# Rotated keys summed on TensorE: cosine and sine part multiplied by the identity into one PSUM bank

## The chip, the cores and the metric

The kernel runs on one core of one Trainium2 chip. The metric is the device time of one execution in microseconds. Three executions of the kernel before took 4159.46 us in the median, 4158.87 us at the least and 4160.84 us at the most.

## What is computed

The input is `x` of shape (8, 512, 128), float32. A modulation vector made from `c` gives shifts, scales and gates. First comes a full attention block with dense 512 x 512 scores for each of the 8 batches. Then comes a stack of six layers, each a windowed attention with rotary positions and a feed-forward part; this stack takes nearly all of the time. Cut to what the change touches:

```python
def attn_layer(x, Wqkv, qs, ksc, Wo):          # x is (8, 512, 128); 16 heads of 64
    q, k, v = split(x @ Wqkv)                  # three times 1024 columns
    q = l2norm(q) * qs
    k = l2norm(k) * ksc
    q = q * cos * scale + rotate_half(q) * sin * scale
    k = k * cos / scale + rotate_half(k) * sin / scale
    out = local_attention(q, k, v)             # windows of 32, each also sees the one before
    return out @ Wo

for i in range(6):
    x = attn_layer(shift_tokens(x), ...) + x
    x = ffn_layer(shift_tokens(x), ...) + x
```

The rotated keys are the sum of a cosine part and a sine part. Tokens lie on partitions when that sum is made, and the scores need the head dimension on partitions, so queries and keys are both turned by TensorE afterwards.

## The kernel before

The stack works on tiles of 128 tokens: 4 tiles in a batch, 32 in a layer, 192 in all. Five engine programs (SyncE, TensorE, ScalarE, GpSimd, VectorE) run side by side and meet only at semaphores. Each is a list of steps per slot, written out by hand for four kinds of slot (`c % 4`). The first slots and the last are unrolled, and the rest is a hardware loop over groups of four slots (`slots`, L276), which goes round 45 times and branches back once for four tiles. A step with lag 2 in slot c works on tile c - 2, so a tile passes through several slots, and each engine's own order decides what can be late.

Per tile, TensorE does six projections (`proj`, L533: chunks 0 and 1 are the queries, 2 and 3 the keys, 4 and 5 the values; each is one float32 matmul of 512 columns into bank 0 or 1). It then does 16 transposes of the rotated queries and keys (`qk_back`, L541: parts 0 and 1 are queries, 2 and 3 keys, four 128 x 128 blocks each, into bank 2 or 5), the mask and 128 small score matmuls (`scores`, L550 and L557), the weighted values (`pv`, L571 and L578, into banks 2 and 5 too) and the output projection (`out_proj`, L589). Once per batch come the centring matmul (L597), transposes of the normalised rows (`norm_back_ffn`, L605), six feed-forward matmuls (`ffn_in`, L613) and three that close it (`ffn_out`, L621).

ScalarE copies the banks out (`to_raw` L1128, `to_v` L1142, `qk_to_sbuf` L1153, `o_to_sbuf` L1164), squares (L1136) and takes the exponentials (L1158) and the gelu (L1187), between which its table is loaded anew. VectorE sums the squares (L1585), scales by the norm (`normed`, L1592), makes the cosine part into `rot` (`cos_part`, L1602) and adds the sine part (`rotated`, L1609), each on 128 x 1024 elements, once for queries and once for keys. It also does the softmax (L1546 to L1571) and the 32 x 32 transpose of the probabilities (`probs_back`, L1578). GpSimd makes the norm's inverse root (L1325, L1327) and the sine part into `swp` (`sin_part`, L1337). SyncE moves the transposed probabilities to a block-diagonal tile `PT` with eight DMAs a tile (`bands`, L356 to L361), for which `pv` waits; `PT` has one buffer, so `bands` also waits for the `pv` of the tile before.

In every slot of the kernel before TensorE runs its steps in nearly this order: `proj` 1 and 3, `qk_back` 1, `out_proj` (lag 4), `qk_back` 0, `proj` 0, `qk_back` 3 and 2, `proj` 4 and 5 (lag 3), `scores` (lag 2), `proj` 2, `pv` (lag 3). In the last kind of slot (`c % 4 == 3`) `norm_back_ffn` follows `pv`, and then the loop turns.

Of the kernel before, what the change touches and what calls it, by code (L numbers as in the profile page):

```python
# [7 lines left out]
ALU = mybir.AluOpType  # L8
# [9 lines left out]
P = 128  # L18
# [49 lines left out]
def adaln_block(nc, x_d, wq_d, wk_d, wv_d, wo_d, bq_d, bk_d, bv_d, bo_d, cT_d, wmod_d,  # L68
# [3 lines left out]
    with ctx:  # L72
# [99 lines left out]
        RAW_BANK = (0, 0, 1, 1, 1, 0)  # L172
# [65 lines left out]
        rot_ready = [sem(f"rot_ready{i}") for i in range(2)]  # L238
# [85 lines left out]
        def _(sp):  # L324
# [68 lines left out]
            def loads_and_moves(l):  # L393
                load_wqkv(l, 1)
                load_wqkv(l, 3)
                load_wqkv(l, 0)
# [3 lines left out]
                move(l, -2)  # L400
                move(l, -1)
                load_wqkv(l, 4)
                load_wqkv(l, 5)
# [22 lines left out]
        def _(pe):  # L426
# [86 lines left out]
            def after(k, c, lag, out):  # L513

                if type(k) is int:
                    wait(pe, out, min(c - lag + 1, NI))
                else:
                    pe.wait_ge(out, k * TPB + (c - lag + 1))

            def after_batch(k, c, lag, out, base=0):  # L520

                b = k + (c // TPB - lag)
                if type(k) is int:
                    if b >= 0:
                        pe.wait_ge(out, min(b, NB - 1) + 1 + base)
                else:
                    pe.wait_ge(out, b + (1 + base))
# [8 lines left out]
            def qk_back(n, b, j, i):  # L536

                pe.wait_ge(rot_ready[i // 2], n + 1)
                for u in range(4):
                    col = (4 * i + u) * P  # L540
                    mm = nc.tensor.transpose(bank[QK_BANK[i]][:, u * P:(u + 1) * P], rot[:, col:col + P], ident[:, :])  # L541
# [82 lines left out]
            def slot(k, c):  # L624
                if c % TPB == 0:
                    if type(k) is int:
                        after(k, c, 1, raw_out[0])
                    if type(k) is int:
                        after(k, c, 1, raw_out[1])
                    after(k, c, 4, v_out[1])  # L630
                    step(k, c, 0, proj, 1, 0)
                    if type(k) is int:
                        after(k, c, 4, v_out[0])
                    if type(k) is int:
                        after(k, c, 1, raw_out[3])
                    after(k, c, 1, raw_out[2])
                    step(k, c, 0, proj, 3, 1)
                    if type(k) is int:
                        after(k, c, 3, qkT_out[3])
                    if type(k) is int:  # L640
                        after(k, c, 3, qkT_out[1])
                    after(k, c, 4, oT_out)
                    step(k, c, 2, qk_back, 1)
                    step(k, c, 4, out_proj)
# [6 lines left out]
                    if type(k) is int:  # L651
                        after(k, c, 4, v_out[1])
                    if type(k) is int:
                        after(k, c, 1, raw_out[0])
                    after(k, c, 0, raw_out[1])
                    step(k, c, 0, proj, 0, 0)
                    if type(k) is int:
                        after(k, c, 4, oT_out)
                    if type(k) is int:
                        after(k, c, 3, qkT_out[3])  # L660
                    after(k, c, 2, qkT_out[1])
                    step(k, c, 2, qk_back, 3)
# [6 lines left out]
                    if type(k) is int:  # L669
                        after(k, c, 1, raw_out[2])  # L670
                    if type(k) is int:
                        after(k, c, 4, v_out[0])
                    after(k, c, 0, raw_out[3])
                    step(k, c, 3, proj, 4, 1)
                    if type(k) is int:
                        after(k, c, 0, raw_out[1])
                    if type(k) is int:
                        after(k, c, 4, v_out[1])
                    after(k, c, 0, raw_out[0])
                    step(k, c, 3, proj, 5, 0)  # L680
# [17 lines left out]
                    step(k, c, 2, scores)  # L698
                    if type(k) is int:
# [15 lines left out]
                    if type(k) is int:  # L715
                        after(k, c, 0, raw_out[3])
                    if type(k) is int:
                        after(k, c, 1, raw_out[2])
                    after(k, c, 3, v_out[0])
                    step(k, c, 0, proj, 2, 1)  # L720
# [16 lines left out]
                    if type(k) is int:  # L737
                        after(k, c, 2, qkT_out[0])
                    if type(k) is int:
                        after(k, c, 4, oT_out)  # L740
                    if type(k) is int:
                        after(k, c, 2, qkT_out[1])
                    after(k, c, 2, qkT_out[2])
                    after(k, c, 2, qkT_out[3])
                    step(k, c, 3, pv)
# [16 lines left out]
                elif c % TPB == 1:  # L762
                    if type(k) is int:
                        after(k, c, 1, raw_out[0])
                    if type(k) is int:
                        after(k, c, 1, raw_out[1])
                    after(k, c, 4, v_out[1])
                    step(k, c, 0, proj, 1, 0)
                    if type(k) is int:
                        after(k, c, 4, v_out[0])  # L770
                    if type(k) is int:
                        after(k, c, 1, raw_out[3])
                    after(k, c, 1, raw_out[2])
                    step(k, c, 0, proj, 3, 1)
                    if type(k) is int:
                        after(k, c, 3, qkT_out[3])
                    if type(k) is int:
                        after(k, c, 3, qkT_out[1])
                    after(k, c, 4, oT_out)
                    step(k, c, 2, qk_back, 1)  # L780
                    step(k, c, 4, out_proj)
                    if type(k) is int:
                        after(k, c, 3, qkT_out[2])
                    if type(k) is int:
                        after(k, c, 3, qkT_out[0])
# [971 lines left out]
```

## Time and profile before

| what | value |
|---|---|
| median of 3 executions | 4159.46 us |
| profiled execution, its own time | 4191.03 us |
| its span, first to last instruction | 4189.0 us |
| mean granted TensorE clock | 0.921 of 2.4 GHz |
| busy share: TensorE, VectorE, GpSimd, ScalarE | 83%, 82%, 66%, 54% |
| first maximum of the softmax (first tile of the stack) | 329.7 us |
| last maximum of the softmax (tile 192) | 4064.3 us |

The profiled execution is 31.6 us (0.8%) longer than the median; shares and durations are read from it, and a change is carried over to the median in proportion. The busy time of TensorE counts modelled ends of matmuls, so what one step costs it is read from the start of one group of matmuls to the start of the next. Idle time of an engine matters only where the end waits for that engine.

### The profile page before, as it was taken

The numbers are of one execution on the slowest core, as the hardware profiler recorded it, in microseconds if no ns is written. First come the engines' busy times: TensorE is split into PE (matmuls) and PEld (weight loads), VectorE is DVE, ScalarE is ACT, GpSimd is POOL, SyncE is SP. The second block draws the span as 40 slices with busy tenths as digits, with TensorE's granted clock in tenths as the row PEclk, the third lists the DMA queues.
The fourth block names the chain that finished last, engine by engine and source line by source line (L and its number), as shares of the span: only waits on it lengthen the run. The fifth ranks groups of instructions, "written<-read, shape, count | busy, mean of one in ns | idle before, by whom it ended". The sixth has DMA issues, their size and how long they took to land. (4 is left out here: it accounts for less than half of the span.)

```text
span 4189.0 us, 120019 instructions
## 1 busy us (share of the span) xinstructions
PE 3460.1 (83%) x45916; PEld 2280.4 (54%) x46108; DVE 3441.1 (82%) x3850; ACT 2249.0 (54%) x3593; POOL 2757.9 (66%) x2144
## 2 busy tenths in 40 slices
PE   4667888888888888888888888888888888888873
PEld 2334555555555555555555555555555555555551
DVE  4658888888888888888888888898898888888871
ACT  2434555555555555555555555555655555655541
POOL 3027767777766776777766767777777767767740
PEclk8779999999999999999999999999999999999985
DMA  1001111111111111111111111111111111111110
GB/s 57 0 0 32 27 27 31 28 37 46 28 27 28 31 37 43 31 27 32 27 37 43 31 27 29 30 37 47 27 31 27 27 39 45 27 31 28 27 32 20
DMA packets 104466, 129.72 MB, mean 31 GB/s; under 512 B 34508, under 2 KB 48208, under 8 KB 104016
## 3 DMA queue, kind: packets, MB, share of 16 engines
q1 hardware_dynamic: 104016, 122.49, 12.0%
q8 instruction: 432, 7.08, 0.7%
q14 instruction: 18, 0.15, 0.0%
HBM read 19.62 MB, written 2.10 MB: 5 GB/s over the span
## 5 line engine op out<-in xcount | busy, mean ns | idle before, releaser
L533 PE MATMUL bank<-wqkv,xs 128*128 128x512 f32 x2304 | 1209.0, 632 | 81.8 <-issue 71.9
L1337 POOL TENSOR_TENSOR swp<-raw,TS 128x512 f32<-128x512 f32 x768 | 960.8, 1272 | 392.4 <-DVE raw L1592 392.1
L1327 POOL TENSOR_TENSOR rr<-ssm,nhalf 128x16 f32<-128x16 f32 x384 | 1176.2, 3063 | 32.0
L1128 ACT ACTIVATE raw<-bank 128x512 f32<-128x512 f32 x768 | 436.9, 597 | 641.2 <-PE bank L533 641.1
L571 PE MATMUL mid<-PT,V 128*64 128x128 f32 x6144 | 462.6, 314 | 298.1 <-DMA PT<-PTd 298.0
L571 PEld LDWEIGHTS mid<-PT,V 128*64 128x64 f32 x6144 | 409.9, 160 | 453.8 <-DMA PT<-PTd 358.9
L533 PEld LDWEIGHTS bank<-wqkv,xs 128*128 128x128 f32 x2304 | 400.1, 197 | 362.6 <-issue 347.7
L1592 DVE TENSOR_TENSOR raw<-raw,rr 128x1024 f32<-128x1024 f32 x384 | 472.0, 1229 | 144.6 <-POOL rr L1327 144.6
L1347 POOL COPY kT<-kT 128x256 f32<-128x256 f32 x192 | 194.7, 1014 | 545.9 <-ACT kT L1153 545.8
L541 PEld LDWEIGHTS mid<-ident,rot 128*128 128x128 f32 x3072 | 379.3, 144 | 248.8 <-issue 228.4
L1609 DVE TENSOR_TENSOR rot<-rot,swp 128x1024 f32<-128x1024 f32 x384 | 468.5, 1220 | 30.1 <-POOL swp L1337 3.5
L1602 DVE TENSOR_TENSOR rot<-raw,TC 128x1024 f32<-128x1024 f32 x384 | 462.0, 1203 | 11.4 <-PE mid L541 10.8
L1585 DVE TENSOR_REDUCE ss<-sq 128x16 f32<-128x1024 f32 x384 | 464.9, 1211 | 5.1 <-ACT sq L1136 5.1
L541 PE MATMUL mid<-ident,rot 128*128 128x128 f32 x3072 | 446.2, 277 | 0.8 <-ACT qT L1153 0.4
L1164 ACT ACTIVATE OT<-mid 128x512 f32<-128x512 f32 x384 | 208.4, 595 | 428.6 <-PE mid L578 296.9
L1136 ACT ACTIVATE sq<-raw 128x1024 f32<-128x1024 f32 x384 | 406.0, 1057 | 29.9 <-DVE ss L1585 14.4
L589 PE MATMUL bank<-OT,fwo 128*128 128x128 f32 x3072 | 381.8, 278 | 3.0 <-ACT OT L1164 3.0
L589 PEld LDWEIGHTS bank<-OT,fwo 128*128 128x128 f32 x3072 | 366.8, 196 | 3.1 <-issue 3.1
L1153 ACT ACTIVATE qT<-mid 128x512 f32<-128x512 f32 x384 | 231.4, 603 | 182.0 <-PE mid L541 182.0
L557 PEld LDWEIGHTS mid<-kT,qT 64*32 64x32 f32 x24576 | 277.5, 105 | 90.1 <-issue 83.6
L613 PE MATMUL bank<-xnT,w 128*128 128x512 f32 (+1 forms) x576 | 315.0, 629 | 8.3 <-ACT ge L1187 4.3
L557 PE MATMUL mid<-kT,qT 64*32 64x64 f32 x24576 | 315.4, 226 | 1.8 <-issue 1.8
(128 smaller groups left out, 4393.1 us busy)
## 6 DMA issues: line engine op xcount, KB each, us to landing
PT<-PTd SPq DMA_DIRECT2D x1344, 64.0 KB
BT<-PTd SPq DMA_DIRECT2D x192, 64.0 KB
wqkv<-d_wqkv SPq DMA_DIRECT2D x36, 256.0 KB, 2.7
fwo<-d_fwo SPq DMA_DIRECT2D x6, 512.0 KB, 4.0
d_out<-X SPq DMA_DIRECT2D x8, 256.0 KB, 2.3
w<-d_w SPq DMA_DIRECT2D x6, 341.0 KB
w<-d_w SPq DMA_DIRECT2D x6, 128.0 KB
wmod<-d_wmod SPq DMA_DIRECT2D x1, 384.0 KB, 3.3
```

Of the source, the lines that this page charges most:

```text
L533: nc.tensor.matmul(bank[bk][:, :], xs[:, j, :], wqkv[:, c, :], start=True, stop=True)\
L541: mm = nc.tensor.transpose(bank[QK_BANK[i]][:, u * P:(u + 1) * P], rot[:, col:col + P], ident[:, :])
L557: mm = nc.tensor.matmul(bank[3 + h][w * W:(w + 1) * W, u * DH:(u + 1) * DH], qT[r, j % 2, u, w * W:(w + 1) * W], kT[r, j % 2, u, w * W:w * ...
L571: mm = nc.tensor.matmul(OUT_BANK[u // 4][h * DH:(h + 1) * DH, (u % 4) * P:(u % 4 + 1) * P], V[:, j % 2, hc:hc + DH], PT[:, :, h * HH + u, ...
L589: mm = nc.tensor.matmul(bank[6][:, j * P:(j + 1) * P], fwo[:, c, :], OT[:, c, :], start=(c == 0), stop=(c == HH - 1), skip_group_check=True)
L1128: nc.scalar.activation(raw[:, j % 2, c * 512:(c + 1) * 512], bank[RAW_BANK[c]][:, :], ACT.Copy)\
L1327: pool.tensor_tensor(rr[:, s], ssm[:, s], nhalf[:, s], ALU.pow).then_inc(rr_ready[i], 1)
L1337: last = pool.tensor_tensor(dst[:, :, t, :], src[:, :, 1 - t, :], tab.broadcast_to([P, HEADS, 32]), ALU.mult)
L1585: nc.vector.tensor_reduce(ss[:, s], sq[:, :].rearrange("p (h d) -> p h d", d=DH), AX.X, ALU.add).then_inc(ss_ready[i], 1)
L1592: nc.vector.tensor_tensor(q, q, rr[:, s].unsqueeze(2).broadcast_to([P, HEADS, DH]), ALU.mult)\
L1602: nc.vector.tensor_tensor(rot[:, i * INNER:(i + 1) * INNER].rearrange("p (h d) -> p h d", d=DH), q, tab.broadcast_to([P, HEADS, DH]), ALU. ...
L1609: nc.vector.tensor_tensor(rot[:, r], rot[:, r], swp[:, r], ALU.add).then_inc(rot_ready[i], 1)
```

## The change

The sum of the rotated keys leaves VectorE. `rotated` stays for the queries; for the keys TensorE multiplies each 128 x 128 block of `rot` by the identity, and then the block of `swp` by the identity into the same place of the same bank, which turns and adds at once. The semaphores follow: `rot_ready` is one, `qk_back` 2 and 3 wait for the cosine and the sine part, and GpSimd's `sin_part` for the keys waits until TensorE has read `swp`.

With it the order of the steps is written anew on every engine. `pv` moves from lag 3 at the end of the slot to lag 4 after the first two projections. `scores` is the last step of TensorE's slot in the kinds 0, 2 and 3, and `norm_back_ffn` goes to the first kind of slot, so that the loop turns right behind `scores`. On ScalarE the exponentials move to lag 3 and the output copy to lag 4. On VectorE the cosine part of the queries and the key norm move to the next slot, ahead of the maximum. On GpSimd the sine part of the queries moves to lag 2. SyncE loads the weight chunks in another order.

```diff
-        RAW_BANK = (0, 0, 1, 1, 1, 0)
+        RAW_BANK = (1, 0, 1, 1, 0, 0)
...
-        rot_ready = [sem(f"rot_ready{i}") for i in range(2)]
+        rot_ready = sem("rot_ready")
...
                 load_wqkv(l, 1)
+                load_wqkv(l, 0)
                 load_wqkv(l, 3)
-                load_wqkv(l, 0)
                 move(l, -4)
                 load_wqkv(l, 2)
                 move(l, -3)
                 move(l, -2)
+                load_wqkv(l, 5)
                 move(l, -1)
                 load_wqkv(l, 4)
-                load_wqkv(l, 5)
...
             def qk_back(n, b, j, i):
 
-                pe.wait_ge(rot_ready[i // 2], n + 1)
+                if i < 2:
+                    pe.wait_ge(rot_ready, n + 1)
+                else:
+                    pe.wait_ge(cos_ready[1], n + 1)
+                    pe.wait_ge(sin_ready[1], n + 1)
                 for u in range(4):
                     col = (4 * i + u) * P
-                    mm = nc.tensor.transpose(bank[QK_BANK[i]][:, u * P:(u + 1) * P], rot[:, col:col + P], ident[:, :])
+                    dst = bank[QK_BANK[i]][:, u * P:(u + 1) * P]
+                    if i < 2:
+                        mm = nc.tensor.transpose(dst, rot[:, col:col + P], ident[:, :])
+                    else:
+                        nc.tensor.matmul(dst, rot[:, col:col + P], ident[:, :], start=True, stop=False)
+                        mm = nc.tensor.matmul(dst, swp[:, col:col + P], ident[:, :], start=False, stop=True)
                 mm.then_inc(qkT_done[i], 1)
```

TensorE's slot of the kind `c % 4 == 3` after the change, its steps alone (the waits for free banks between them are left out); the kind 2 is the same without `centred`:

```python
step(k, c, 0, proj, 1, 0)
step(k, c, 0, proj, 0, 1)
step(k, c, 4, pv)
step(k, c, 3, proj, 5, 0)
step(k, c, 0, proj, 3, 1)
step(k, c, 2, qk_back, 3)
step(k, c, 2, qk_back, 0)
step(k, c, 4, out_proj)
step(k, c, 2, qk_back, 1)
step(k, c, 2, qk_back, 2)
step(k, c, 3, proj, 4, 0)
batch(k, c, 1, centred)
step(k, c, 0, proj, 2, 1)
step(k, c, 2, scores)
```

The kind 0 has `norm_back_ffn` (lag 2) after `pv`, and `ffn_in` 0 of the gate between `proj` 2 and `scores`. The kind 1 has the other five `ffn_in` after `proj` 1, `proj` 0, `pv`, `proj` 3 and `qk_back` 2, and `ffn_out` after `scores`.

```diff
             def sin_part(n, b, j, i):
 
                 pool.wait_ge(qn_ready[i], n + 1)
-                wait(pool, rot_ready[i], n)
+                if i == 0:
+                    wait(pool, rot_ready, n)
+                else:
+                    for c in (2, 3):
+                        wait(pool, qkT_done[c], n)
...
             def rotated(n, b, j, i):
                 dve.wait_ge(sin_ready[i], n + 1)
                 dve.wait_ge(cos_ready[i], n + 1)
-                r = slice(i * INNER, (i + 1) * INNER)
-                nc.vector.tensor_tensor(rot[:, r], rot[:, r], swp[:, r], ALU.add).then_inc(rot_ready[i], 1)
+                r = slice(0, INNER)
+                nc.vector.tensor_tensor(rot[:, r], rot[:, r], swp[:, r], ALU.add).then_inc(rot_ready, 1)
```

The other engines' slots after the change, kind 2, steps alone (ScalarE, GpSimd, VectorE):

```python
to_raw 1, to_raw 0, exps (lag 3), o_to_sbuf (lag 4), squares 0, qk_to_sbuf 3, qk_to_sbuf 0 (lag 2),
to_raw 3, to_v 5 (lag 3), qk_to_sbuf 1, qk_to_sbuf 2 (lag 2), to_raw 2, to_v 4 (lag 3), squares 1
take_x, sin_part 0, sin_part 1 (lag 2), norms 0 (lag 1), keys_before (lag 2), norms 1 (lag 1)
sumsq 0, cos_part 0, normed 1, rotated 0 (lag 1), maxes, less_max (lag 2), cos_part 1 (lag 1),
sumsq 1, sums, sums_inverse, probs (lag 2), normed 0, probs_back (lag 2), x_between
```

In the kind 0 ScalarE's three gelus stand at the end of its slot, behind `squares` 1.

## Rows read from the trace of the kernel before

**Rows 1.** The page, busy time: us, share of span, instructions, of TensorE.

```profile
PE 3460.1 (83%) x45916; PEld 2280.4 (54%) x46108; DVE 3441.1 (82%) x3850; ACT 2249.0 (54%) x3593; POOL 2757.9 (66%) x2144
```

**Rows 2.** Windows, the stack: length, busy of PE, PEld, DVE, ACT, POOL, clock, DMA.

```profile
330.00:4064.00 3734.00, 3227.49 (x45037) 2153.89 (x45227) 3241.18 (x3370) 2105.14 (x3322) 2673.10 (x1994) 0.95 0.14 32
```

**Rows 3.** Waits of TensorE: who waited for whom, us in total, times, longest.

```profile
PE mid L571 <- DMA PT<-PTd: 298.0, 114, 6.3
PE bank L533 <- issue: 71.9, 49, 2.7
PE mid L550 <- ACT kT L1153: 66.5, 51, 5.5
...
PE bank L621 <- DVE ge L1640: 35.1, 47, 1.3
```

**Rows 4.** Groups by line: shapes, count, busy us and mean ns, idle before.

```profile
L1609 DVE TENSOR_TENSOR rot<-rot,swp 128x1024 f32<-128x1024 f32 x384 | 468.5, 1220 | 30.1 <-POOL swp L1337 3.5
...
L1128 ACT ACTIVATE raw<-bank 128x512 f32<-128x512 f32 x768 | 436.9, 597 | 641.2 <-PE bank L533 641.1 <-DVE rot L1602 0.2
...
L1136 ACT ACTIVATE sq<-raw 128x1024 f32<-128x1024 f32 x384 | 406.0, 1057 | 29.9 <-DVE ss L1585 14.4
...
L589 PE MATMUL bank<-OT,fwo 128*128 128x128 f32 x3072 | 381.8, 278 | 3.0 <-ACT OT L1164 3.0
...
L1187 ACT ACTIVATE ge<-bank,b 128x512 f32<-128x512 f32 x144 | 98.8, 686 | 108.6 <-PE bank L613 108.0
...
L1187 ACT ACT_TABLE_LOAD x48 | 61.6, 1283 | 0.8
```

**Rows 5.** Timeline of TensorE's matmuls, 2054 to 2058 us: start, length, line, count.

```profile
2054.20 1.95 PE L589 MATMUL bank<-OT,fwo 128*128 128x128 f32 x16
2055.98 0.60 PE L541 MATMUL mid<-ident,rot 128*128 128x128 f32 x4
2056.42 1.02 PE L533 MATMUL bank<-wqkv,xs 128*128 128x512 f32 x2
2057.28 1.04 PE L541 MATMUL mid<-ident,rot 128*128 128x128 f32 x8
```

**Rows 6.** Line 276, the loop: ns min/median/max, first and last start; PEldq, ACTq sequencers.

```profile
L276 PEldq COMPARE_BRANCH  x45: 76/3557/3887, 580.1 to 4027.7; - x45
...
L276 ACTq COMPARE_BRANCH  x45: 40/45/45, 582.2 to 4030.7; - x45
```

**Rows 7.** Timeline of TensorE around the loop's first turn.

```profile
578.66 2.84 PE L571 MATMUL mid<-PT,V 128*64 128x128 f32 x28
581.43 0.66 PE L605 MATMUL bank<-ident,xn 128*128 128x128 f32 x4
583.89 1.59 PE L533 MATMUL bank<-wqkv,xs 128*128 128x512 f32 x2 [1.81 <-issue]
```

**Rows 8.** Timeline of TensorE, end of a slot of kind 3 and the next.

```profile
2536.84 0.38 PE L550 MATMUL mid<-maskb,identb 128*128 128x512 bf16 x1 [0.33 <-issue]
2537.15 1.58 PE L557 MATMUL mid<-kT,qT 64*32 64x64 f32 x128
2538.66 1.13 PE L533 MATMUL bank<-wqkv,xs 128*128 128x512 f32 x2
2543.59 3.63 PE L571 MATMUL mid<-PT,V 128*64 128x128 f32 x32 [3.81 <-DMA PT<-PTd]
...
2549.64 2.98 PE L533 MATMUL bank<-wqkv,xs 128*128 128x512 f32 x4 [1.83 <-issue]
```

**Rows 9.** Windows: `pv` after that wait; columns as in Rows 2.

```profile
2543.60:2546.90 3.30, 3.30 (x32) 3.25 (x32) 3.20 (x3) 1.06 (x1) 3.13 (x3) 0.51 0.03 5
```

**Rows 10.** Timeline of VectorE: the probabilities' transpose, and two steps in a row.

```profile
2534.94 1.25 DVE L1578 STREAM_TRANSPOSE PTd<-Pr 128x1024 f32<-128x1024 f32 x1
...
2597.39 1.22 DVE L1592 TENSOR_TENSOR raw<-raw,rr 128x1024 f32<-128x1024 f32 x1
2598.53 1.21 DVE L1585 TENSOR_REDUCE ss<-sq 128x16 f32<-128x1024 f32 x1
```

## What I predicted, and how it was worked out

> **What bounds the kernel now.** I first read the page's busy shares: TensorE and VectorE are both at 82% to 83%, GpSimd at 66%, so neither of the first two can be taken for the bound by its share [rows 1]. Over the stack alone, 3734 us, TensorE is busy 3227 us and VectorE 3241 us, 86% and 87% [rows 2]. TensorE therefore has 507 us in which its array does nothing, and that is the number against which this change must be held, since the change gives TensorE work and takes it from VectorE.
>
> The waits say where these 507 us lie [rows 3]. `pv` waits 298 us for the DMAs that fill `PT`, the loop's first projection 72 us for "issue", the mask matmul before `scores` 67 us for the key copy, and the last feed-forward matmul 35 us for VectorE. The timeline shows one such end of slot: `scores`, a projection, then 3.81 us of nothing until `pv`, and 1.83 us more before the next slot's projection [rows 8]. Between these stalls TensorE is gapless. So it is a chain through TensorE (scores, softmax on VectorE, eight DMAs, `pv`, then TensorE's next slot) that sets the period, with TensorE 86% full.
>
> The granted clock is 0.95 over the stack [rows 2]. The levels are 2.4 and 1.2 GHz, so 3734 x 0.05 x 2 = 373 us ran at the lower one. It falls behind the long wait: after the 3.81 us gap the `pv` ran at 0.51 for 3.3 us [rows 8, 9].
>
> **The keys' work on TensorE.** Eight key blocks a tile were one transpose each; now each is two float32 matmuls. What a transpose costs is read between starts: four from 2055.98 to 2056.42, 0.110 us each [rows 5]. For the new matmul the nearest row is `out_proj`, with the same shape: 128x128 stationary, 128 columns moving, float32. It has 3072 instructions for 192 x 8 matmuls, so two per matmul, and 16 of them took 2054.20 to 2055.98, 0.111 us each [rows 4, 5]. A block now costs 4 x 0.111 = 0.445 us in place of 0.110. That is 0.335 us more, and with 192 x 8 = 1536 blocks **+515 us**. From the other side, if float32 times the identity went through in one instruction as a transpose does, a block would cost 0.222 us and the term would be +172 us. I take +515, by the row of equal kind.
>
> **The addition taken from VectorE.** 192 of the 384 executions of line 1609 go, at 1.14 us from start to start (1.22 us long, overlapping) [rows 4, 10]: 219 us of VectorE. I cost them at nothing. VectorE would have 3241 - 219 = 3022 us of work in a stack that TensorE alone fills for longer; this takes more idle from VectorE than there was, but no wait of TensorE that the new order would not also take.
>
> **The new order.** `pv` of a tile ran one slot after its scores; now it runs early in the second. After `scores` come on VectorE nine steps and a reciprocal until `probs_back` ends, about 10.2 us by 1.14 to 1.25 us each [rows 4, 10]. From the end of `probs_back` (2536.19) to the waiting `pv` it took 7.4 us, DMA issue and landing together [rows 8, 10]. So `pv` could start 17.6 us after `scores` ends. TensorE reaches it after one whole slot and two projections of 0.86 us [rows 5]. A plain slot now sums to 16.7 us: six projections (5.2), `pv` (3.0: its first 32 matmuls half of the 3.63 us at the lower clock, and an estimated 1.1 for the 32 small ones, whose price lies between the 0.012 us of a score matmul and the 0.057 us of a wide one), two key parts (3.56), two query parts (0.88), `out_proj` (1.78), `scores` with the mask (2.3) [rows 5, 8]. That makes 18.4 us, later than 17.6, and the slots with feed-forward work are longer. So **-298 us**, with a cover of only 0.8 to 2 us in plain slots; if VectorE comes late, part returns. The mask's wait for the key copy goes too, since two projections now stand between the last key part and `scores`. Of its 66.5 us, 51 x 0.33 us stay, a gap that the row shows without any wait [rows 3, 8]: **-50 us**. The last feed-forward matmul now stands behind `scores`, with its input ready: **-35 us** [rows 3]. The other waits in the new slot I covered one by one. The bank copies of 0.60 us lie behind `pv`, `out_proj` or two projections. `qk_back` 3 needs the cosine part made four steps after the previous `scores` ended, before the slot's first five steps (6.5 us) are over. `sin_part` and `keys_before` have GpSimd's spare third.
>
> The gelus lose cover. The first follows `proj` 2 on ScalarE by a copy, another copy, squares, a table load and itself: 0.60 + 0.60 + 1.06 + 1.28 + 0.69 us [rows 4], with 0.4 us of hand-over 4.6 us. TensorE has 0.9 (`ffn_in`) + 2.3 + 0.9 us = 4.1 us to fill, and waits 0.5 us. The second gelu has one projection, 0.86 us, against 0.69 + 0.4 us, and costs 0.25 us. With 48 batches this makes **+36 us**, between 0 and +60. The weight loads in another order cost nothing: each has most of a slot before its chunk is used, as before. Pipeline fill and drain have the same 8 slots; I leave 10 us either way for them.
>
> **The turn of the loop.** TensorE's sequencer takes 3.56 us (median of 45) for the loop's branch, ScalarE's 0.045 us [rows 6]. In the first turn the branch started at 580.1 and the next projection at 583.89, 3.8 us later. Work already queued covered part: the rest of `pv` and the four transposes, up to 582.1, so 1.81 us stood open [rows 6, 7]; the mean is 71.9 / 45 = 1.6 us. Wide work hid the rest. In the new order the branch follows `scores`, 128 matmuls in 1.5 us, 0.012 us each [rows 8]. A queue holding the same 18 matmuls or so that still ran during the old turn (four transposes and 14 of `pv`) now hides 0.2 us. So 3.6 us stand open, 2.0 us more, 45 times: **+90 us**. The bounds are 0, if the branch is reached as early in time as now, and +100.
>
> The Trainium skill (Runtime: NRT & Kernel Launch, Instruction fetch mechanics) says that a taken branch whose target lies outside the two pages of instructions at hand waits for a DMA fetch; the 3.56 us on TensorE against 0.045 us on ScalarE agree. Another page of the Trainium skill (Advanced Engine Details and Errata, Control Flow Timing) gives a compare-and-branch 108 ns; here TensorE's trace contradicts it.
>
> **The clock.** Today the low stretches cost about half of 373 us where TensorE works, 86% of it: 160 us. They follow the `pv` gaps, which go: **-160 us**. But the new gap of 3.6 us at the turn is nearly the 3.81 us behind which the clock fell. I take it that it falls for 3.4 us once in a turn, as in rows 9, and half of that is lost: 45 x 1.7 = **+76 us**, between 0 and +150.
>
> The Trainium skill (TensorE: Matmul & The Clock Gate, Part 4) holds that transposes do not count as activity for the clock as matmuls do. By it the change feeds the clock, and the +76 us would be 0; no row here parts the two.
>
> **The sum:** 515 - 298 - 50 - 35 + 36 + 90 - 160 + 76 = +174 us. On 4191.03 us of the profiled execution this gives 4365 us, and on the median 4159.46 x 4365 / 4191.03 = **4332 us**, 4.1% slower. The change fills TensorE's idle time and then some.
>
> **Rivals.** *The turn costs TensorE nothing* (the other side). If the branch took no array time, its +90 and +76 and today's 72 us would go: 174 - 90 - 76 - 72 = -64 us, 4096 us. It decides from the point where less than about 1.4 us of a turn stands open. Control Flow Timing, named above, would give this. Against it stand 45 turns of the same length. With one instruction a matmul (+172 in place of +515) the sum is -169 us, 3992 us, but two rows of instructions per matmul speak against it. Together 0.08.
>
> *The turn stays as now and the clock holds:* 174 - 90 - 76 = +8 us, 4167 us, no change. Chance 0.05. *Only one of the two holds:* +84 to +98 us, 4243 to 4257 us. Chance 0.17.
>
> *`PT` comes late again.* The cover is 0.8 to 2 us in plain slots, and VectorE's own order has waits for TensorE in it (the gated products in the kind 0 slot wait for `ffn_in` while the softmax stands behind them). With 2 us lost in two slots of each batch, +190 us: 174 + 190 = +364 us, 4521 us; with a half of it 4426 us. Chance 0.20.
>
> *The change doesn't do what it says:* if VectorE kept 384 additions, nothing of the sum would change but VectorE's load; the diff leaves no room for it.
>
> **How the numbers follow.** Forecast, 4332 us, with its own range 4290 to 4385: 0.50. No more than 2 in 10 may be left out: I go from 4190, above the cases of no change and of the other side (0.13), to 4470, which takes most of the late-`PT` case. About 0.2% is what a measurement of this kernel can tell from no change. Faster: 0.08. Same: 0.05. Slower: 0.50 + 0.17 + 0.20 = 0.87.
>
> **What would show it.** In the changed kernel's groups by line, line 1609 has 192 executions, and the key matmuls have 6144 instructions, near 0.111 us from start to start. TensorE's busy share over the stack rises to nine tenths. Its waits hold little on `PT`, and "issue" before the first projection is near 45 x 3.6 = 160 us. The granted clock is below 1 once in four tiles, behind the turn. I am wrong if `PT` waits stay above 100 us, if the turn is as open as before, or if the key matmuls go at half the price.

## The result

| kernel | median | against the kernel before, same chip |
|---|---|---|
| before | 4160.15 us (4 runs, that chip) | |
| changed | 4359.5 us (4357.85 to 4362.37) | 1.0474 [1.0455, 1.0493] |

The change makes the kernel 4.7% slower. The profiled execution of the changed kernel took 4359.32 us, with a span of 4357.3 us against 4189.0 us: 168 us more. Between the medians it is 199 us, since the profiled execution of the kernel before was 31.6 us above its median and that of the changed kernel was at its own.

From its page, the busy times, and from the windows one window of the stack (length, busy PE, PEld, DVE, ACT, POOL, clock, DMA share, GB/s). These answer rows 1 and 2:

```profile
PE 3910.7 (90%) x50716; PEld 2736.4 (63%) x50716; DVE 3412.3 (78%) x3658; ACT 2249.5 (52%) x3593; POOL 2848.1 (65%) x2144
...
330.00:4064.00 3734.00, 3472.57 (x47033) 2461.74 (x47033) 3033.89 (x3002) 1990.75 (x3141) 2616.97 (x1890) 0.97 0.13 31
```

TensorE went from 86% to 93% of the stack and VectorE from 87% to 81%. TensorE's waits in the changed kernel, answering rows 3 (us in total, times, longest):

```profile
PE bank L534 <- issue: 175.9, 48, 5.4
PE mid L581 <- DMA PT<-PTd: 59.0, 53, 5.2
...
PE bank L623 <- ACT ge L1197: 20.1, 48, 1.1
PE mid L550 <- ACT OT L1174: 20.0, 36, 0.9
...
PE mid L567 <- issue: 8.5, 21, 0.9
...
PE bank L631 <- DVE ge L1654: 1.3, 1, 1.3
```

The wait for `PT` fell from 298 to 59 us, those before the mask and the last feed-forward matmul are gone, and the turn of the loop rose from 72 to 176 us. Its place in TensorE's timeline (start, length, line, count), the branch's own line (ns min, median, max; first and last start), and two windows, the empty array and the projection after the turn, answering rows 6 to 9:

```profile
2565.99 1.93 PE L567 MATMUL mid<-kT,qT 64*32 64x64 f32 x128
2571.82 3.58 PE L534 MATMUL bank<-wqkv,xs 128*128 128x512 f32 x4 [3.90 <-issue]
...
L276 PEldq COMPARE_BRANCH  x45: 76/3602/5071, 570.3 to 4240.7; - x45
...
570.80:574.00 3.20, 0.00 (x0) 0.00 (x0) 3.20 (x3) 0.06 (x1) 3.04 (x3) 1.00 0.10 26
574.50:578.00 3.50, 3.50 (x10) 1.24 (x11) 3.50 (x3) 1.61 (x5) 3.33 (x4) 0.55 0.02 5
```

The branch lasts as long as before, 3.60 us, and nothing stands over it. After it the clock is at its lower level, 1.2 GHz, for a stretch.

The matmuls that were added, from the timeline of one key part, which answers rows 5:

```profile
2561.07 0.39 PE L550 MATMUL mid<-ident,rot 128*128 128x128 f32 x2
2561.29 0.39 PE L551 MATMUL mid<-ident,swp 128*128 128x128 f32 x2
...
2562.63 0.39 PE L551 MATMUL mid<-ident,swp 128*128 128x128 f32 x2
2562.85 1.02 PE L534 MATMUL bank<-wqkv,xs 128*128 128x512 f32 x2
```

Sixteen instructions from 2561.07 to 2562.85, 0.111 us each.

One difference lies outside the stack. At the end, the chain that ended last (start, us, what) shows this in the kernel before and then in the changed one:

```profile
4130.23 44.07 issue
4174.30 1.10 PE bank L1056 x4
```

```profile
4342.28 0.30 issue
4342.59 1.10 PE bank L1066 x4
```

In those 44 us the trace of the kernel before holds 404 semaphore instructions on TensorE's queue and no matmul. All but one are waits that `after` and `after_batch` emit in unrolled slots whose steps have run out, each long satisfied, one every 0.109 us. In the diff of the change these two helpers have new conditions, `if c - lag < NI` and `if 0 <= b < NB`, which no longer emit them. So the stack itself became 168 + 44 = 212 us longer, not 168. From the first to the last maximum of the softmax it is 3735 us before and 3953 us (325.1 to 4277.9) after.

### The profile page after: what moved, and what is told of

Its sections match the earlier page's. It is cut to its first block and busy times, and to the rows that moved or that the text cites. A ratio compares the mean times of both kernels' runs of the same rounds, so it can differ in the third digit from the quotient of the medians.

```text
span 4357.3 us, 128635 instructions
## 1 busy us (share of the span) xinstructions
PE 3910.7 (90%) x50716; PEld 2736.4 (63%) x50716; DVE 3412.3 (78%) x3658; ACT 2249.5 (52%) x3593; POOL 2848.1 (65%) x2144
## 5 line engine op out<-in xcount | busy, mean ns | idle before, releaser
L534 PE MATMUL bank<-wqkv,xs 128*128 128x512 f32 x2304 | 1200.8, 639 | 179.8 <-issue 175.9
L1351 POOL TENSOR_TENSOR swp<-raw,TS 128x512 f32<-128x512 f32 x768 | 1119.4, 1487 | 0.4 <-DVE raw L1606 0.4
L1327 POOL COPY xs<-F 128x128 f32 (+1 forms) x192 | 178.1, 928 | 1051.2 <-issue 856.7
L1623 DVE TENSOR_TENSOR rot<-rot,swp 128x1024 f32<-128x1024 f32 x192 | 386.3, 2012 | 410.2 <-POOL swp L1351 410.2
L550 PE MATMUL mid<-ident,rot 128*128 128x128 f32 x3072 | 600.4, 277 | 26.2 <-ACT OT L1174 20.0
L551 PE MATMUL mid<-ident,swp 128*128 128x128 f32 x3072 | 595.9, 276 | 0.0
L550 PEld LDWEIGHTS mid<-ident,rot 128*128 128x128 f32 x3072 | 479.1, 192 | 135.6 <-issue 70.0
L581 PEld LDWEIGHTS mid<-PT,V 128*64 128x64 f32 x6144 | 355.7, 144 | 238.8 <-issue 152.8
L1163 ACT ACTIVATE kT<-mid 128x512 f32<-128x512 f32 x384 | 229.3, 597 | 481.0 <-PE mid L551 481.0
L551 PEld LDWEIGHTS mid<-ident,swp 128*128 128x128 f32 x3072 | 468.4, 193 | 0.0
L581 PE MATMUL mid<-PT,V 128*64 128x128 f32 x6144 | 402.3, 287 | 59.0 <-DMA PT<-PTd 59.0
L623 PE MATMUL bank<-xnT,w 128*128 128x512 f32 (+1 forms) x576 | 311.5, 623 | 25.0 <-ACT ge L1197 20.1
```

The lines of the kernel that those rows point to most:

```text
L534: nc.tensor.matmul(bank[bk][:, :], xs[:, j, :], wqkv[:, c, :], start=True, stop=True)\
L550: nc.tensor.matmul(dst, rot[:, col:col + P], ident[:, :], start=True, stop=False)
L551: mm = nc.tensor.matmul(dst, swp[:, col:col + P], ident[:, :], start=False, stop=True)
L581: mm = nc.tensor.matmul(OUT_BANK[u // 4][h * DH:(h + 1) * DH, (u % 4) * P:(u % 4 + 1) * P], V[:, j % 2, hc:hc + DH], PT[:, :, h * HH + u, ...
L1351: last = pool.tensor_tensor(dst[:, :, t, :], src[:, :, 1 - t, :], tab.broadcast_to([P, HEADS, 32]), ALU.mult)
```

## The experiments

The theory on record: TensorE binds the changed kernel; its work, the open turn and the clock behind the turn cost time one to one. The general rival: the new order of steps, or another engine, sets the time. The order of the sections is that in which the runs were made; each group of sections that names one comparison ran against its own runs of the kernel before, so ratios are compared, and a difference of ratios is given in us of 4160.

The 44 us at the end must be kept apart. The kernels made from the kernel before (it and the experiments 4, 8 and 11) have them, all the others don't. Where the two sorts are compared, 44 us (0.011) of the difference of the ratios is not the sum of the keys and not the order of the stack. The profiles give the stack alone, from the first to the last maximum:

| kernel | stack, us |
|---|---|
| before | 3735 |
| changed | 3953 |
| addition back, new order | 3831 |
| matmuls, old order | 3907 |
| before, loop written out | 3729 |
| changed, loop written out | 3742 |
| addition back, new order, loop written out | 3747 |
| matmuls, old order, loop written out | 3812 |
| all three together | 3558 |

### The turn moved behind wide work

```diff
-            slots(pe, 8, slot)
+            slots(pe, 10, slot)
```

> The changed kernel with TensorE's loop shifted by two slots, so that it turns behind ffn_out (six wide matmul instructions, 2.65 us) and no longer behind scores. No work is added or left out. My theory: the turn stands open on TensorE's path. In the changed kernel 45 turns wait 175.9 us in all, 3.9 us each; behind ffn_out about 2.5 us of each should be hidden (-112 us), and with an opening of about 1.4 us the clock should mostly not fall behind it (about -60 us): near 4190 us, between 4170 and 4260. Rival, the turn lies beside other waits (the order of the other engines sets the period): no change, 4340 to 4370 us.

Measured: 4293.68 us, 1.0286 [1.0265, 1.0307]. That is 0.0188 less than the changed kernel, 78 us. Half of what I expected.

```profile
PE bank L534 <- issue: 122.4, 78, 2.5
...
PE mid L550 <- ACT OT L1174: 33.7, 88, 1.0
PE bank L615 <- ACT xn L1183: 32.9, 41, 4.4
...
L276 PEldq COMPARE_BRANCH  x44: 83/4384/4748, 611.7 to 4137.4; - x44
```

The first three rows are TensorE's waits, the last the branch. The turn does lie on the path, so the rival falls. But the branch itself now lasts 4.38 us instead of 3.60, and two ScalarE waits that the long stall had covered came out.

### The keys' cosine part alone

```diff
-                        nc.tensor.matmul(dst, rot[:, col:col + P], ident[:, :], start=True, stop=False)
-                        mm = nc.tensor.matmul(dst, swp[:, col:col + P], ident[:, :], start=False, stop=True)
+                        mm = nc.tensor.transpose(dst, rot[:, col:col + P], ident[:, :])
```

> The changed kernel, but TensorE makes four transposes of rot a key part as the kernel before did and leaves the keys' sine part out of the result; all waits stay. It takes away the added TensorE work alone (0.335 us a block, 515 us in all) and adds nothing elsewhere. My theory, TensorE's work is the bound: the time falls by 515 us until something else binds. A plain slot would be 14.0 us, and pv can start only 17.6 us after scores; one slot and two projections are then 15.7 us, so some 1.9 us of waiting for PT come back in most slots, about +240 us: near 4085 us, between 3900 and 4130. Rival, the order of the steps on VectorE and GpSimd made the changed kernel slow and the matmuls are hidden: above 4300 us.

Measured: 4123.45 us, 0.9879 [0.9858, 0.9899]; 248 us less than the changed kernel for 515 us less TensorE work. Its waits and its branch:

```profile
PE bank L534 <- issue: 214.3, 49, 5.4
PE mid L580 <- DMA PT<-PTd: 175.5, 52, 5.0
...
L276 PEldq COMPARE_BRANCH  x45: 76/4590/5130, 558.5 to 4006.6; - x45
```

The time is inside my range. The added work is on the path, and the cover of `PT` that I had put at 0.8 us in plain slots is thin: with 2.7 us less work a tile, 116 us of waiting for `PT` return. Another 38 us went into a longer branch. The granted clock of the stack was 0.94 (330 to 4050 us) in place of 0.97, which is 0.03 x 2 x 3720 = 223 us more at the lower level, half of it lost: some 110 us. With these three, what is left of the 515 us is the 248 us measured.

### The addition back on VectorE, in the new order

```diff
+                pe.wait_ge(rot_ready[i // 2], n + 1)
...
+                        mm = nc.tensor.transpose(dst, rot[:, col:col + P], ident[:, :])
...
                     step(k, c, 1, cos_part, 1)
+                    step(k, c, 1, rotated, 1)
```

> The changed kernel's order of steps, but the keys' sum is made as in the kernel before: an addition on VectorE right behind the keys' cosine part, then transposes. My theory: as with the cosine part alone, but the addition (1.15 us) stands between the maximum and the probabilities of the same slot and lengthens the way from scores to pv: near 4200 us, between 4080 and 4280, so faster than the changed kernel by TensorE's 515 us less what comes back as waiting. Rival, the new order itself is what costs: 4360 us or more, since VectorE has more to do.

Measured: 4237.62 us, 1.0160 [1.0132, 1.0188].

```profile
PE bank L534 <- issue: 217.6, 52, 5.1
PE mid L576 <- DMA PT<-PTd: 187.3, 55, 4.8
PE mid L546 <- DVE rot L1614: 59.3, 52, 3.3
```

As expected: in the new order the matmuls cost 131 us more than the addition that they replace. Even so this kernel stays slower than the kernel before, so the new order alone, with the same arithmetic, costs 1.6%. In the stack it costs more, 97 us (3831 against 3735), since only the kernel before has the 44 us at the end. The waits show where: 218 us before the loop's first projection, in place of 72. A part of that is a longer branch, 4.67 us in the median.

### The matmuls in the old order

```diff
-                pe.wait_ge(rot_ready[i // 2], n + 1)
+                if i < 2:
+                    pe.wait_ge(rot_ready[0], n + 1)
+                else:
+                    pe.wait_ge(cos_ready[1], n + 1)
+                    pe.wait_ge(sin_ready[1], n + 1)
...
-                    step(k, c, 1, rotated, 1)
```

> The kernel before with its own order of steps and its own place of the loop's turn, but with the keys' sum made by the matmuls and VectorE's addition for the keys gone. My theory: TensorE's added 515 us first fill its waits for PT (298 us) and keep the clock up (up to 160 us): near 4220 us, between 4180 and 4350, so faster than the changed kernel by about what the open turn and the clock behind it cost. Rival, only the new order makes room for the matmuls: 4360 us or more.

Measured: 4371.03 us, 1.0475 [1.0447, 1.0504]. My expectation failed: the whole time is the changed kernel's, not 140 us less. But this kernel has the 44 us at the end, and its stack is 46 us shorter than the changed kernel's (3907 against 3953), a third of what I expected.

```profile
PE bank L533 <- issue: 115.6, 49, 3.0
PE mid L559 <- ACT kT L1162: 62.8, 51, 1.8
PE mid L566 <- issue: 50.7, 43, 2.0
...
PE mid L580 <- DMA PT<-PTd: 25.5, 24, 6.3
```

The first half of the thought was right: the wait for `PT` fell from 298 to 26 us. But the waits before `scores` stay, 63 us for the key copy. There are 51 us of new idle time within the score matmuls, 43 times, at places where the program has no wait (why was not tried). And the turn opens wider, 116 us in place of 72. The new order removes those waits and pays for it with a turn of 176 us and the clock behind it; with the loop it loses 46 us by this in the stack, and only the shorter end of the program makes the two times equal.

### TensorE's loop written out

```diff
+        class K(int):
+            pass
...
+            for k in range(1, groups):
+                for i in range(TPB):
+                    body(K(k), lag + i)
...
-            slots(pe, 8, slot)
+            unrolled(8, slot)
```

> The changed kernel with TensorE's loop written out: the same steps and waits in the same order with constants in place of the register, and no turn at all; the other engines keep their loops. My theory: the 176 us of open turns and the some 70 us of lower clock behind them are on the path. With the turn only moved, about 50 us came back as waits for ScalarE (the output copy and the normalised rows), so I expect near 4165 us, between 4100 and 4210. Rival, the sequencer must fetch the same instructions anyway and the stall moves into the straight code: above 4290 us.

Measured: 4143.51 us, 0.9912 [0.9895, 0.9928]. TensorE's waits in the stack and the window of it:

```profile
PE mid L594 <- issue: 56.2, 57, 1.7
...
PE mid L594 <- DMA PT<-PTd: 14.5, 9, 5.9
...
330.00:4000.00 3670.00, 3539.82 (x48868) 2529.20 (x48868) 3156.17 (x3124) 2059.53 (x3266) 2797.38 (x1966) 1.00 0.13 32
```

234 us less than the changed kernel, and inside my range. The projections wait 2.0 us in all for issue in place of 176, the clock is 1.00 over the stack, and TensorE is busy 96%. The turns with the clock behind them are the whole of the slowdown. (The edit also takes the register arithmetic off TensorE's queue. It was not tried alone, but outside the turns the changed kernel's TensorE waited only some 10 us for issue.) But without them the change doesn't make the stack faster either: it takes 3742 us against 3735. The 0.9% (37 us) by which the whole kernel is faster than the kernel before is no more than the 44 us at the end.

### Half the price for a key block

```diff
-                        nc.tensor.matmul(dst, rot[:, col:col + P], ident[:, :], start=True, stop=False)
-                        mm = nc.tensor.matmul(dst, swp[:, col:col + P], ident[:, :], start=False, stop=True)
+                        nc.tensor.transpose(dst, rot[:, col:col + P], ident[:, :])
+                        mm = nc.tensor.matmul(dst, swp[:, col:col + P], ident[:, :], start=False, stop=True,
+                                              skip_group_check=True)
```

> The changed kernel, but the cosine part of a key block is transposed (one instruction) and only the sine part is multiplied by the identity onto it (two). The whole result is computed. A block costs 0.109 + 0.223 = 0.332 us in place of 0.446, 175 us less in all. My theory, the time follows TensorE's work one to one: near 4190 us, between 4160 and 4260. Rival, at this load waits between the engines take over: above 4290 us.

Measured: 4292.97 us, 1.0270 [1.0253, 1.0287]; 85 us less than the changed kernel, not 175.

```profile
PE bank L534 <- issue: 231.6, 48, 5.7
PE mid L582 <- DMA PT<-PTd: 80.5, 52, 5.2
...
L276 PEldq COMPARE_BRANCH  x45: 76/5020/5475, 562.6 to 4174.8; - x45
```

This is outside my range of 4160 to 4260 and just inside the rival's, but it was not mainly waits between the engines that took over. The branch grew to 5.02 us, and that ate 56 us; 22 us went into waiting for `PT`, and the granted clock of the stack was 0.96 in place of 0.97. By the two waits alone 97 us of the 175 us are left, 12 more than measured.

### The addition back, loop written out

The third experiment and the fifth together; no further edit.

> The changed kernel's order with VectorE's addition and the transposes, and TensorE's loop written out. With the loop it took 4238 us, 218 us of it open turns and some 60 us of clock behind them, 187 us waits for PT. My theory: the turns' time goes, and a third of it comes back as waiting for PT: near 4050 us, between 3950 and 4130, faster than the kernel before. Rival, VectorE's chain from scores to pv sets the period and the turn lies inside its shadow: above 4190 us.

Measured: 4158.31 us, 0.9955 [0.9938, 0.9971]: 85 us less than with the loop, well above my 4050 and outside my range, but below the rival's 4190.

```profile
PE mid L589 <- issue: 181.0, 95, 4.1
PE mid L559 <- DVE rot L1627: 136.9, 97, 3.3
PE bank L631 <- DVE ge L1658: 66.6, 49, 1.8
```

Here TensorE waits again: before `pv`, which needs `PT`, and for VectorE before the query parts and the feed-forward matmuls. VectorE is busy 3401 of the 3670 us from 330 to 4000, 93%, and TensorE 87%; VectorE in its turn waits 173 us for GpSimd's sine part, so that VectorE alone binds is likely but not shown. Without turns matmuls (0.9912) and addition (0.9955) are nearly equal in the new order.

### The kernel before, loop written out

The fifth experiment's edit on the kernel before.

> The kernel before with TensorE's loop written out, nothing else changed. Its turns are open 72 us in all and the clock falls again behind a half of them. My theory: the turn stands on the chain through TensorE here too: near 4080 us, between 4040 and 4120. Rival, the wait for PT is the fixed point and takes the gain: within 10 us of the kernel before.

Measured: 4182.33 us, 0.9994 [0.9976, 1.0012]. The rival held.

```profile
PE mid L584 <- issue: 307.8, 123, 4.7
...
PE mid L584 <- DMA PT<-PTd: 36.9, 12, 7.9
```

The waits before `pv` rose from 298 to 345 us. The 72 us of open turns in the kernel before cost nothing: 47 us of them reappear before `pv`, and 37 us of idle time appear within the score matmuls, where there was 2 us.

### Half the price, loop written out

The fifth and the sixth together.

> The changed kernel with TensorE's loop written out, and each key block as one transpose of the cosine part and one matmul of the sine part onto it. The whole result is computed. Without turns the first gain of 175 us can't be eaten by a longer turn. My theory: against the 4144 us of the unrolled kernel, the 175 us go and some 40 us come back as waits for PT and for ScalarE: near 4010 us, between 3960 and 4070, faster than both kernels. Rival, something else already binds the unrolled kernel beside TensorE (VectorE's chain, as in the unrolled kernel with the addition, 4158 us): above 4110 us.

Measured: 4029.89 us, 0.9661 [0.9637, 0.9684], 104 us less than unrolled alone and inside my range.

```profile
PE mid L595 <- issue: 102.9, 86, 2.1
...
PE mid L595 <- DMA PT<-PTd: 17.6, 8, 5.6
```

With no branch to grow, the cheaper block pays, less 50 us that come back before `pv` (121 us against 71).

### The keys' sine part after the queries' addition

VectorE's additions had become longer. The changed kernel's line, what VectorE waited for before it (us, times), and one tile from the timelines of TensorE, VectorE and GpSimd:

```profile
L1623 DVE TENSOR_TENSOR rot<-rot,swp x192: 1209/2268/2285, 307.1 to 4258.2; 128x1024 f32<-128x1024 f32 x192
...
  POOL swp L1351: 410.2, 155
...
2546.86 1.48 PE L567 MATMUL mid<-kT,qT 64*32 64x64 f32 x128
...
2549.61 2.29 DVE L1623 TENSOR_TENSOR rot<-rot,swp 128x1024 f32<-128x1024 f32 x1 [2.64 <-POOL swp L1351]
...
2560.39 1.24 DVE L1592 STREAM_TRANSPOSE PTd<-Pr 128x1024 f32<-128x1024 f32 x1
...
2547.08 5.95 POOL L1351 TENSOR_TENSOR swp<-raw,TS 128x512 f32<-128x512 f32 x4
```

The addition starts when the queries' sine part is done, and at that moment GpSimd starts the keys'. There is a second thing in these lines. In the kernel before the addition waited 3.5 us in all for GpSimd; now, with the queries' sine part moved to lag 2, it waits 410 us. In this tile the scores end at 2548.34, the addition starts 1.3 us later and takes 2.29 us, and `probs_back` ends at 2561.63. That is 13.3 us after the scores, where I had counted 10.2. The experiment parts the addition from the keys' sine part, which starts later by it; the addition's wait for GpSimd stays (407 us).

```diff
                 if i == 0:
                     wait(pool, rot_ready, n)
                 else:
+                    pool.wait_ge(rot_ready, n + 1)
                     for c in (2, 3):
                         wait(pool, qkT_done[c], n)
```

> The changed kernel with TensorE's loop written out, and one wait more on GpSimd: the keys' sine part starts only when the queries' addition on VectorE is done. In the changed kernel the two run side by side in most tiles and take 2.27 us each, against 1.22 and 1.27 us alone. My theory: the addition falls to 1.22 us, and the time stays within 15 us of the unrolled kernel's (4144 us), since TensorE binds. Rival, VectorE's lost microsecond a tile is on the path: 4100 us or less.

Measured: 4083.28 us, 0.9784 [0.9759, 0.9809], 53 us less than unrolled alone. The rival held.

```profile
L1637 DVE TENSOR_TENSOR rot<-rot,swp x192: 1210/1226/1227, 306.9 to 3990.2; 128x1024 f32<-128x1024 f32 x192
...
PE mid L594 <- issue: 17.3, 28, 1.8
...
PE mid L594 <- DMA PT<-PTd: 11.0, 6, 5.4
```

The addition is back at 1.23 us, and the waits before `pv` fell by 42 us (56.2 + 14.5 against 17.3 + 11.0). The additions became 151 us shorter in all (192 of 2.01 us in the mean against 192 of 1.22), and 53 us of that arrived. So VectorE's time between `scores` and `probs_back` reaches TensorE in part, through `PT`, even when TensorE is busy 96% of the time. What the wait for GpSimd costs was not tried.

### The matmuls in the old order, loop written out

The fourth and the fifth together.

> The kernel before in its own order, the keys' sum by matmuls, TensorE's loop written out. With the loop it took 4371 us, 116 us of it before the loop's first projection. My theory after the last runs: with TensorE's added work it is TensorE that binds in this order too, so the turns count here though they did not in the kernel before: near 4250 us, between 4210 and 4290, and thus slower than the new order unrolled (4144 us) by its waits for the key copy. Rival, its own order's waits take the gain as in the kernel before: above 4330 us.

Measured: 4275.64 us, 1.0252 [1.0226, 1.0278], inside my range.

```profile
PE mid L593 <- issue: 101.7, 82, 2.5
PE mid L572 <- ACT kT L1175: 62.9, 51, 1.8
```

93 us less than with the loop, where the kernel before gained nothing from the same edit: with the matmuls TensorE binds in the old order too. Without turns the whole kernel in the new order is 0.034, 141 us, faster. In the stack it is 70 us (3742 against 3812), about the 63 us of waits for the key copy; the 44 us at the end, which this kernel still has, are most of the rest.

### All three together

> The changed kernel with TensorE's loop written out, one transpose and one matmul a key block, and the keys' sine part on GpSimd held until the queries' addition is done. The whole result is computed. Without the last the kernel took 4030 us, with 103 us of issue waits and 18 us of DMA waits before pv. My theory: the collision of VectorE and GpSimd delays the probabilities, and through PT it costs TensorE some 45 to 90 us here, since TensorE has less work to hide it: near 3970 us, between 3940 and 4000. Rival, at this load the later sine part is late for the key blocks and eats the gain: 4020 us or more.

Measured: 3962.66 us (5 runs), 0.9538 [0.9523, 0.9553], 4.6% faster than the kernel before and inside my range. It is 0.0123, 51 us, less than without the held sine part. Of the 190 us, 44 us are again the end of the program; the stack is 177 us shorter (3558 against 3735).

```profile
330.00:3860.00 3530.00, 3395.87 (x47697) 2384.07 (x47885) 3090.50 (x3163) 2070.96 (x3304) 2835.97 (x1987) 1.00 0.14 34
```

TensorE is still busy 96% of the stack, so little but its own work is left there.

## Why the prediction held, point by point

I forecast 4332 us, between 4190 and 4470; 4359.5 us were measured. The steps, by the profiled executions:

| step | forecast, us | measured, us | from |
|---|---|---|---|
| key blocks on TensorE | +515 | +515 (0.111 us an instruction) | timeline |
| wait for `PT` | -298 | -239 | waits |
| waits before `scores` | -50 | at most -106 (114 to 8.5), see below | waits |
| last feed-forward matmul | -35 | -34 | waits |
| gelus | +36 | +16 (4.3 to 20.1) | waits |
| output copy before the key part | 0 | +20 | waits |
| turn of the loop | +90 | +104 | waits |
| clock, old low stretches less new | -84 | -77 | clock records |
| tail's satisfied waits | not seen | -44 | chain |

The clock's entry comes from the trace's records of the granted clock, added up over the stack. They give 399 us at the lower level before and 225 us after, and TensorE's matmuls fill 356 and 202 us of them. Half of that is lost: 178 us before, 101 us after. Worked out as in the prediction, from the mean clock rounded to 0.95 and 0.97, it would be 160 and 104.

*The sum.* That the forecast of +174 us and the 168 us between the profiles lie so near is partly luck. With the waits before `scores` at -66 (below) the measured entries add up to +195, and 27 us stay unexplained. Against my terms, the waits for `PT` brought 59 us more, the output copy 20, the turn 14 and the clock 7; the tail brought 44 us less, the gelus 20 and the waits before `scores` 16. And the profiled execution of the kernel before was 31.6 us above its median: between the medians I forecast +173 us, and +199 us were measured.

*The key blocks.* Right to the thousandth of a us, and the row of `out_proj` was the right one. The second experiment shows that they lie on the path.

*The wait for PT.* Its direction was right. The term that was mis-sized is the cover: I put every VectorE step behind `scores` at its length in the kernel before, and without a wait. One that stands just ahead of the maximum, the queries' addition, became 2.27 us long in most tiles. I had looked for collisions nowhere. The tenth experiment shows that this made up 42 us of waits before `pv` in the unrolled kernel. The same addition also waits for GpSimd's sine part, 410 us in 155 tiles, where I had written that `sin_part` has GpSimd's spare third. What this wait costs TensorE was not tried and stays open.

*Waits before scores.* I let 0.33 us stay as a gap without a wait. The trace of the kernel before holds 192 mask matmuls of 384, the changed one all, so a part of that gap was a missing record. The row's fall of 106 us is therefore too much by the matmuls not recorded, some 40 us at 0.2 us each, estimated.

*The turn.* Forecast 3.6 us open, measured 175.9 / 45 = 3.9. The mechanism was right and the experiments show its weight: 234 us with the clock behind it, net of the waits that come out without it. That the clock falls behind it was right too: every one of the 44 gaps of more than 3.3 us at the loop's turn in the stack is followed by a low stretch, and the unrolled kernel has a clock of 1.00. I had put this at 76 us; it is the 101 us above.

*What bounded the kernel before.* This sentence was wrong. I wrote that a chain through TensorE, with its next slot in it, set the period. The eighth experiment took 72 us of TensorE's idle time away and the kernel was as fast as before (0.9994). The sum survived since it counted only TensorE's own time after the change, when TensorE does bind. Which chain sets the period of the kernel before stays open; the seventh experiment, where the same addition on VectorE makes TensorE wait in three places, points to VectorE's side but belongs to the new order of steps.

*The tail.* I read the chain that ended last only as far as the stack and passed over its 44 us. That the `after` edit is the cause was not tried alone; all four kernels with the old helpers show a wait of 47 us before these transposes, and none of those with the new ones does.

*The rivals.* "The turn costs TensorE nothing" was priced at 4096 us. The unrolled kernel realises it: 0.9912 x 4160 = 4123 us. That the price is only 27 us off is luck too: the 44 us of the tail, which no price had, are in it, and without them it would be 4167 us, 71 us above the price. While the loop stands the rival didn't hold. "`PT` comes late again" held in a small part, 59 us.

## What to carry to other kernels

An engine that is 86% busy gains nothing by work that adds 14%, however well the other engine is relieved: with the loop written out and nothing else changed the stack came out as long as before. Count the added instructions against the idle time of the engine that receives them, with the cost read from start to start. Look at what an order of steps puts next to a loop's branch: here four slots of TensorE's instructions make a branch of some 4 us, 45 times, and writing the loop out was worth 234 us to the changed kernel and nothing to the kernel before. When two kernels differ in more than one thing, compare the stretch that matters and not only the whole: here 44 us at the end of the program passed for a gain of the change. When a transpose and an addition are joined on TensorE, transpose the first part and multiply only the second onto it.

## What I had not expected of the hardware

- The branch of TensorE's loop has no fixed price. The medians are 3.56 us (before), 3.60 (changed), 3.69 (matmuls in the old order), 4.38 (turn moved), 4.59 (cosine part alone), 4.67 (addition back) and 5.02 us (half price). In the new order, all three bodies that are shorter than the changed kernel's had a longer branch. Why was not tried.
- A VectorE addition with two float32 inputs and a GpSimd multiplication with two, run side by side, take 2.27 us each in place of 1.22 and 1.27, not far from the sum of both. Beside GpSimd's power (2.93 us) the same addition kept its 1.22 us in the kernel before. The Trainium skill (GPSIMD Engine Reference, Specifications) says that GpSimd's SBUF interfaces are shared with VectorE, with contention for VectorE instructions that have two SBUF inputs; the trace agrees and gives it a size.
- A transpose writes a bank and a matmul then accumulates onto it: 1.0270 against 1.0474 with the loop, 0.9661 against 0.9912 without.
- A satisfied wait on TensorE's queue costs about 0.11 us: the 404 semaphore instructions at the end of the kernel before took 44 us.
